# GpSimd splits four fifths of every tap group, SyncE alone moves the first two batches

## The chip, the cores and the metric

The kernel runs on one core of a Trainium2 chip. The metric is the device time of one execution in microseconds (us); the median of three runs before the change is 339.46 us. The question is what the change does to that time.

## The reference, cut to what matters

x has the shape 16 x 128 x 32 x 32 in float32. Two blocks follow each other, each on a group-normalised input, each added to its input:

```
t1 = einsum('nchw,he->ncew', gn(x), p1)                 # 16 rows e out of 32 rows h
t3 = depthwise conv 9x9 of t1 with p3                   # the "taps"
t4 = grouped conv (5 x 1, groups of 4 channels) with p4 # "mix"
t5 = einsum('ncew,ewf->ncf', t4, p5)                    # f = 3 * 128
t6 = depthwise conv of t5 along f with p6
x1 = x + einsum('ncf,nfp->ncp', t6, shifted rows of gn(x)) / sqrt(3c)
out = x1 + relu(batch_norm(1x1 conv of [g2, upsampled Haar details of g2])),  g2 = gn(x1)
```

Products are made at nearly float32 accuracy: each factor is written as a high part (a cast to fp32r) and a rest ("low", the float32 value minus the high part), and three products high x high, high x low, low x high are summed in PSUM.

## The kernel before, in words

The first stage (to about 42 us) loads x, transposes it on VectorE and multiplies it by p1 (`t1`). The second stage, the convolution, runs over 32 channel groups g of four channels. For each group a weight block `s_f` of 128 x 768 is loaded by SyncE's queue (five taps of 128 columns and one mix block of 128 columns), ScalarE casts it to `s_hi` (L516), and the rest `s_lo` is a subtraction. In groups 0 to 13 (`LO_POOL` = 14) GpSimd makes the rest of columns 0 to 511 (`taps_low`, L411) and VectorE that of the other 256 (`split_low`, L859); from group 14 on VectorE makes all 768 columns. Each weight group is split two groups ahead of its use, so in step g of ScalarE and of VectorE group g + 2 is split. `s_lo` and `s_hi` have three buffers, `s_f` has six.

TensorE does for a group fifteen matmuls (L718): ten with `s_hi`, then five with `s_lo`, for which it waits until both parts of the rest are there (`taps_split`). Then come the three mix matmuls of the group before (`t4_product`, L247 to L249, called t4 below), which need `t3_hi` (ScalarE, L558) and `t3_lo` (VectorE, L879) of that group. ScalarE's order within a step g: `t3_hi` of g, evacuation of t4 of g - 1 (L543), the cast `s_hi` of g + 2, and then extras. VectorE's: `t3_lo` of g, the rest of g + 2, extras.

The extras: the evacuated t4 tiles are regrouped by transfers from SBUF to SBUF (`shuffle`, L302) in four batches of 9, 9, 9 and 5 groups, 16 blocks each, and then split (`d_high` on ScalarE L551 or on GpSimd L407; `d_low` on VectorE L868, 128 x 612). For batches 0 to 2 SyncE issues 8 blocks and GpSimd 8, for batch 3 it is 7 and 9. SyncE does so in its loop of weight loads, for batch 0 in its steps 18 to 21 and for batch 1 in steps 27 to 30, two blocks in each; its step g waits for the rest of group g - 6 before it loads the weights of group g. ScalarE's first `d_high` of batch 0 stands in step 15, that of batch 1 in step 25, and each waits for the whole batch (`wait_d`). Other extras are the statistics of x on VectorE (L840, L892, L898, and the group averages, one matmul L728 on TensorE ahead of the next group), the split of p5 (`p5_lo`, L911), a power -1/2 on GpSimd (L437) and the forms of the 1x1 weights on GpSimd (`w_forms`, L417 to L422).

After group 31 batches 2 and 3 are split: all four pieces of each on ScalarE and VectorE. TensorE bridges this time with matmuls that only keep its clock (L750), and then starts the product with p5 (`t5_product`), whose first part needs twelve pieces of the first three batches and the first of batch 3. The third stage runs over the 16 images, and the last one applies the batch normalisation and stores.

Of the kernel before, what the change touches and what calls it, by code (L numbers as in the profile page):

```python
# [38 lines left out]
NB, GB = 4, 9  # L39
# [11 lines left out]
WR, SR = 6, 3  # L51
# [1 line left out]
BY_ACT = 1  # L53
ACT_STATS = {2: (0, 0), 5: (0, 1)}
EARLY = 8
LO_POOL, LO_COLS = 14, 4 * C
AGGR_AT, ST1_AT, GST_AT = 13, 17, 20
P5_AT, P5_LO_AT = 7, {9: 0, 10: 1, 11: 2, 12: 3}
P5_RAW_AT = 6
W_RAW_AT, W_DET_AT = 21, 16  # L60
SHUFFLE_AT = (18, 27)
SHUFFLE_POOL_AT = 10
PER_STEP = 2
SP_BLOCKS, LAST_SP = 8, 7
D_HI_AT = {15: (0, 0), 18: (0, 1), 20: (0, 2), 22: (0, 3), 25: (1, 0), 28: (1, 1)}
D_HI_POOL = ((1, 2), (1, 3))
D_LO_AT = {16: (0, 0), 19: (0, 1), 21: (0, 2), 23: (0, 3), 26: (1, 0), 27: (1, 2), 29: (1, 1), 30: (1, 3)}
D_HI_ACT = list(D_HI_AT.values()) + [(b, piece) for b in (NB - 2, NB - 1) for piece in range(CI)]


def build(nc, x, p1_blk_in, taps_in, p5_in, p6, w_in, gamma, beta, out):
    ctx = ExitStack()
    with ctx:
# [218 lines left out]

        def wait_d(eng, b):

            by_pool = len(blocks) - (SP_BLOCKS if b < NB - 1 else LAST_SP)
            eng.wait_ge(d_in[b], 16 * (len(blocks) - by_pool))
            eng.wait_ge(d_in_pool[b], 16 * by_pool)

        def shuffle(eng, b, some, done):
            groups = FIRST[b + 1] - FIRST[b]  # L300
            for jl, co in some:
                eng.dma_start(  # L302
                    d_sb[b][32 * jl:32 * jl + 32, co].rearrange("p g j n -> p (g j n)"),
                    t4_out[32 * co:32 * co + 32, b % 2, jl, 0:groups].rearrange("p g j n -> p (g j n)")
                    ).then_inc(done, 16)

        def d_ready(eng, b):

            eng.wait_ge(s["t4_ev"], FIRST[b + 1])
            eng.wait_ge(s["conv"], d_groups[b])  # L310

        @block.sync
        def _(sp):
# [17 lines left out]
            def shuffle_step(step):  # L331

                for b in range(NB - 2):
                    i = PER_STEP * (step - SHUFFLE_AT[b])
                    if i == 0:
                        d_ready(sp, b)
                    if 0 <= i < SP_BLOCKS:
                        shuffle(sp, b, blocks[i:i + PER_STEP], d_in[b])

            for g in range(3, G):  # L340
# [8 lines left out]
                    sp.wait_ge(s["p5_lo"], JC)  # L349
                    sp.dma_start(w_raw[:, :, :], w_in).then_inc(s["w_raw"], 16)  # L350
            d_ready(sp, NB - 2)
            shuffle(sp, NB - 2, blocks[:SP_BLOCKS], d_in[NB - 2])
            sp.wait_ge(s["d_lo"], CI)
            sp.wait_ge(s["conv"], x_groups)
            reload_x(sp, 0)
# [15 lines left out]
        def _(pool):  # L371
# [42 lines left out]
            def w_forms():  # L414
                pool.wait_ge(s["w_det"], 1)
                w1, w2, w3, minus_w1 = (w_det[:, k, :] for k in range(4))
                pool.tensor_tensor(w_f[:, 1, :], w2, w3, ALU.add)  # L417
                link(pool.tensor_tensor(w_f[:, 3, :], w2, w3, ALU.subtract))
                pool.tensor_tensor(w_f[:, 2, :], w1, w_f[:, 1, :], ALU.subtract)
                link(pool.tensor_tensor(w_f[:, 4, :], minus_w1, w_f[:, 3, :], ALU.subtract))  # L420
                pool.tensor_tensor(w_f[:, 1, :], w1, w_f[:, 1, :], ALU.add)
                pool.tensor_tensor(w_f[:, 3, :], minus_w1, w_f[:, 3, :], ALU.add).then_inc(s["w_f"], 1)  # L422

            def two_blocks(b, i):
                shuffle(pool, b, blocks[SP_BLOCKS + 2 * i:SP_BLOCKS + 2 * i + 2], d_in_pool[b])
# [410 lines left out]
        def _(dve):  # L836
# [281 lines left out]
```

## Time and profile before

| what | value |
|---|---|
| three runs | 338.56, 339.46, 340.72 us |
| the profiled execution, its time | 337.9 us |
| its span, first to last instruction | 336.1 us |
| mean granted TensorE clock | 0.927 |
| TensorE matmul busy | 274.3 us (82%) |
| VectorE busy | 277.9 us (83%) |
| ScalarE busy | 231.4 us (69%) |
| GpSimd busy | 207.2 us (62%) |

The times of single instructions below are of the profiled execution, in us from the start of its span; 1.8 us of its time lie outside the span. Busy shares are averages over stages with different limits, so the argument goes by the rows of the convolution.

### The profile page before, as it was taken

The numbers are of one execution on the slowest core, as the hardware profiler recorded it, in microseconds if no ns is written. First come the engines' busy times: TensorE is split into PE (matmuls) and PEld (weight loads), VectorE is DVE, ScalarE is ACT, GpSimd is POOL, SyncE is SP. The second block draws the span as 40 slices with busy tenths as digits, with TensorE's granted clock in tenths as the row PEclk, the third lists the DMA queues.
The fourth block names the chain that finished last, engine by engine and source line by source line (L and its number), as shares of the span: only waits on it lengthen the run. The fifth ranks groups of instructions, "written<-read, shape, count | busy, mean of one in ns | idle before, by whom it ended". The sixth has DMA issues, their size and how long they took to land.

```text
span 336.1 us, 4816 instructions
## 1 busy us (share of the span) xinstructions
PE 274.3 (82%) x1544; PEld 226.7 (67%) x1544; DVE 277.9 (83%) x541; ACT 231.4 (69%) x353; POOL 207.2 (62%) x203
## 2 busy tenths in 40 slices
PE   3576599979899889999999999999999998871000
PEld 0111189979799885878888998988889997750000
DVE  3899878997779697768789999999999999765992
ACT  0797838855787657547657778787777787464990
POOL 7398866790029915215878888888898888642000
PEclk9978969998999999999999999999999999987555
DMA  8999456577668376792000000000000000000599
GB/s 216 313 319 277 160 194 184 186 206 208 194 197 245 83 231 168 277 412 102 2 0 3 0 1 2 0 0 2 0 4 1 0 2 0 0 0 1 234 405 360
DMA packets 15096, 43.59 MB, mean 130 GB/s; under 512 B 3056, under 2 KB 3280, under 8 KB 15072
## 3 DMA queue, kind: packets, MB, share of 16 engines
q1 hardware_dynamic: 12672, 36.83, 33.2%
q10 hardware_dynamic: 1344, 4.20, 4.3%
q0 software_dynamic: 1056, 2.27, 2.3%
q8 instruction: 12, 0.20, 0.2%
q14 instruction: 12, 0.10, 0.1%
HBM read 30.44 MB, written 8.39 MB: 116 GB/s over the span
## 4 chain that ended last, share of the span: by engine, by line
PE 54%; DVE 18%; ACT 8%; POOL 6%; DMA 5%; issue 5%; SPq 1%; DVEq 0%; POOLq 0%; ACTq 0%
PE wide L718 10%; PE wide L247 9%; PE wide L249 8%; PE wide L248 8%; DVE xa L853 5%; DVE x_sb L1066 5%; PE bank L795 4%; PE bank L247 4%; PE bank L249 3%; PE bank L248 3%; DMA x_slot<-in_x 3%; DMA d_sb<-t_out 2%; PE bank L799 2%; DVE s_lo L859 2%; DVE d_split L868 2%
## 5 line engine op out<-in xcount | busy, mean ns | idle before, releaser
L718 PE MATMUL wide<-t_all,s_hi 128*128 128x272 f32 (+1 forms) x320 | 47.5, 297 | 2.2 <-ACT t_all L507 1.4
L718 PEld LDWEIGHTS wide<-t_all,s_hi 128*128 128x128 f32 x320 | 43.9, 202 | 3.5 <-ACT t_all L507 2.3
L475 POOL TENSOR_TENSOR g_lo<-y_sb,g_hi 128x1024 fp32r<-128x1024 f32 x15 | 36.1, 2409 | 14.5 <-ACT y_sb L645 14.5
L451 POOL TENSOR_TENSOR g_lo<-y_sb,g_hi 128x1024 fp32r<-128x1024 f32 x15 | 36.0, 2399 | 12.1 <-ACT g_hi L605 12.1
L247 PE MATMUL wide<-g_hi,t_hi 128*128 128x512 f32 x96 | 37.5, 390 | 0.3 <-DVE t_lo L985 0.3
L249 PE MATMUL wide<-g_hi,t_lo 128*128 128x512 f32 x96 | 37.6, 392 | 0.0
L248 PE MATMUL wide<-g_lo,t_hi 128*128 128x512 f32 x96 | 37.4, 390 | 0.0
L853 DVE STREAM_TRANSPOSE xa<-x_slot 128x1024 f32<-128x1024 f32 x16 | 31.3, 2023 | 6.9 <-DMA x_slot<-in_x 6.2
L644 ACT ACTIVATE g_hi<-x_sb,rs 128x1024 fp32r<-128x1024 f32 x16 | 21.3, 1330 | 19.9 <-POOL rs L460 19.9
L859 DVE TENSOR_TENSOR s_lo<-s_f,s_hi 128x768 fp32r<-128x768 f32 (+1 forms) x32 | 25.5, 796 | 9.9 <-ACT s_hi L516 9.7
L302 POOL DMA_DIRECT2D d_sb<-t_out x33 | 16.6, 508 | 26.3 <-ACT t_out L543 26.1
L397 POOL TENSOR_TENSOR t_all<-t_f,t_all 128x512 fp32r<-128x512 f32 x17 | 26.0, 1556 | 8.8 <-ACT t_f L510 8.7
L686 PE MATMUL bank<-xa,p_blk 128*64 128x512 f32 x64 | 21.2, 754 | 10.5 <-DVE xa L853 7.9
L516 ACT CAST s_hi<-s_f 128x768 fp32r<-128x768 f32 x32 | 26.7, 834 | 0.0
L958 DVE TENSOR_TENSOR x_sb<-x_sb,wide 128x512 f32<-128x512 f32 x32 | 21.7, 678 | 5.8 <-PE wide L249 5.8
L558 ACT CAST t_hi<-wide 128x272 fp32r<-128x272 f32 x32 | 12.6, 393 | 19.5 <-PE wide L718 19.5
L718 PE MATMUL wide<-t_all,s_lo 128*128 128x272 f32 (+1 forms) x160 | 25.6, 291 | 0.1
L247 PE MATMUL bank<-p_hi,d_split 128*128 128x384 f32 x68 | 24.6, 362 | 0.7 <-DVE d_split L868 0.7
L411 POOL TENSOR_TENSOR s_lo<-s_f,s_hi 128x512 fp32r<-128x512 f32 x14 | 20.4, 1459 | 7.9 <-ACT s_hi L516 7.8
L686 PEld LDWEIGHTS bank<-xa,p_blk 128*64 128x64 f32 x64 | 3.8, 154 | 28.5 <-DVE xa L853 28.0
L249 PE MATMUL bank<-p_hi,d_split 128*128 128x384 f32 x68 | 23.0, 338 | 0.0
L248 PE MATMUL bank<-p_lo,d_split 128*128 128x384 f32 x68 | 22.9, 337 | 0.0
(136 smaller groups left out, 833.7 us busy)
## 6 DMA issues: line engine op xcount, KB each, us to landing
s_f<-in_taps SPq DMA_DIRECT2D x32, 384.0 KB, 4.0
x_sb<-in_x SPq DMA_DIRECT2D x8, 1024.0 KB, 8.0
out<-x_sb SPq DMA_DIRECT2D x7, 1024.0 KB, 5.1
x_slot<-in_x ACTq DMA_DIRECT2D x12, 256.0 KB, 13.5
x_slot<-in_x SPq DMA_DIRECT2D x12, 256.0 KB, 14.1
d_sb<-t_out POOLq DMA_DIRECT2D x24, 76.5 KB, 3.3
d_sb<-t_out SPq DMA_DIRECT2D x24, 76.5 KB, 3.2
x_slot<-in_x ACTq DMA_DIRECT2D x8, 128.0 KB, 4.6
```

Source lines behind the costliest of these rows:

```text
L247: nc.tensor.matmul(ps, w[0], m[0], start=start, stop=False)
L248: nc.tensor.matmul(ps, w[0], m[1], start=False, stop=False)
L249: return nc.tensor.matmul(ps, w[1], m[0], start=False, stop=stop)
L397: pool.tensor_tensor(t1[:, :, 1, 2:2 + J, at].rearrange("p g j -> p j g"), t1_f[i % 2][:, :, :], t1[:, :, 0, 2:2 + J, at].bitcast(F32).rea ...
L451: pool.tensor_tensor(g1_lo[:, W:W + HW], y_sb[:, n, :], g1_hi[:, W:W + HW].bitcast(F32), ALU.subtract).then_inc(s["g1_lo"], 1)
L475: pool.tensor_tensor(g2_lo[:, :], y_sb[:, n, :], g2_hi[:, :].bitcast(F32), ALU.subtract).then_inc(s["g2_lo"], 1)
L516: act.copy(s_hi[:, g % SR, :], s_f[:, g % WR, :]).then_inc(s["s_hi"], 1)
L686: mm = pe.matmul(ps_t1[i % 4][64 * v:64 * v + 64, :], p1_blk[:, :], rhs, start=True, stop=True)
L718: mm = pe.matmul(ps_t3[g % 2][:, j0 * NO:j1 * NO], weights[:, g % SR, 128 * t:128 * t + 128], t1_all[:, row + j0:row + j1, :].rearrange("p ...
L853: dve.transpose(xa[:, n % 2], x_slot[n // 2][:, n % 2, :].rearrange("p (h w) -> p w h", w=W)).then_inc(s["xa"], 1)
L859: dve.tensor_tensor(s_lo[:, g % SR, first:], s_f[:, g % WR, first:], s_hi[:, g % SR, first:].bitcast(F32), ALU.subtract).then_inc(s["s_lo" ...
L958: dve.tensor_tensor(x_sb[:, n, sl], x_sb[:, n, sl], ps_o[:, sl], ALU.add).then_inc(s["x1"], 1)
```

## The change

GpSimd's loop `for g in range(G)` now covers all 32 groups of `taps_low`; VectorE makes the rest of columns 512 to 767 alone, in all groups. SyncE issues all 16 blocks of batches 0 and 1, four in each of its steps 18 to 21 and 27 to 30. GpSimd's other work is put into its loop: `w_forms` behind group 23, the two `d_high` behind groups 27 and 29, the power behind group 30; its shares of batches 2 and 3 come behind the loop. The aggregation of the statistics moves from step 13 to 17, its last part from 17 to 21 (TensorE's average from ahead of group 19 to ahead of group 23), the factors from 20 to 24; `p5_lo` from steps 9 to 12 to steps 12 to 15; the load of the 1x1 weights from SyncE's step 21 to 24 and their scaling on ScalarE from step 16 to 19; `d_low` of piece (1, 2) from step 27 to 28.

```diff
-LO_POOL, LO_COLS = 14, 4 * C
-AGGR_AT, ST1_AT, GST_AT = 13, 17, 20
-P5_AT, P5_LO_AT = 7, {9: 0, 10: 1, 11: 2, 12: 3}
+LO_COLS = 4 * C
+AGGR_AT, ST1_AT, GST_AT = 17, 21, 24
+P5_AT, P5_LO_AT = 7, {12: 0, 13: 1, 14: 2, 15: 3}
 P5_RAW_AT = 6
-W_RAW_AT, W_DET_AT = 21, 16
+W_RAW_AT, W_DET_AT = 24, 19
 SHUFFLE_AT = (18, 27)
-SHUFFLE_POOL_AT = 10
-PER_STEP = 2
-SP_BLOCKS, LAST_SP = 8, 7
+PER_STEP = 4
+SP_BLOCKS, LAST_SP = (16, 16, 8), 7
+POW_AT, W_FORMS_AT = 30, 23
 D_HI_AT = {15: (0, 0), 18: (0, 1), 20: (0, 2), 22: (0, 3), 25: (1, 0), 28: (1, 1)}
-D_HI_POOL = ((1, 2), (1, 3))
-D_LO_AT = {16: (0, 0), 19: (0, 1), 21: (0, 2), 23: (0, 3), 26: (1, 0), 27: (1, 2), 29: (1, 1), 30: (1, 3)}
+D_HI_POOL_AT = {27: (1, 2), 29: (1, 3)}
+D_HI_POOL = list(D_HI_POOL_AT.values())
+D_LO_AT = {16: (0, 0), 19: (0, 1), 21: (0, 2), 23: (0, 3), 26: (1, 0), 28: (1, 2), 29: (1, 1), 30: (1, 3)}
...
-            eng.wait_ge(s["s_lo_pool"], min(g + 1, LO_POOL))
+            eng.wait_ge(s["s_lo_pool"], g + 1)
...
-            for g in range(LO_POOL):
+            for g in range(G):
                 taps_low(g)
-                if g == SHUFFLE_POOL_AT:
-                    d_ready(pool, 0)
-                if g >= SHUFFLE_POOL_AT:
-                    two_blocks(0, g - SHUFFLE_POOL_AT)
-            d_ready(pool, 1)
-            for i in range(2):
-                two_blocks(1, i)
-            pool.wait_ge(s["gst"], 1)
-            pool.tensor_tensor(rs1[:, 1, :], rs1[:, 0, :], minus_half[:, :].broadcast_to([128, N]),
-                               ALU.pow).then_inc(s["gst_q"], 1)
-            for i in range(2, 4):
-                two_blocks(1, i)
-            w_forms()
-            for b, co in D_HI_POOL:
-                d_high(b, co)
-            d_ready(pool, 2)
-            shuffle(pool, 2, blocks[SP_BLOCKS:], d_in_pool[2])
-            d_ready(pool, 3)
-            shuffle(pool, 3, blocks[LAST_SP:], d_in_pool[3])
+                if g in D_HI_POOL_AT:
+                    d_high(*D_HI_POOL_AT[g])
+                if g == W_FORMS_AT:
+                    w_forms()
+                if g == POW_AT:
+                    pool.wait_ge(s["gst"], 1)
+                    pool.tensor_tensor(rs1[:, 1, :], rs1[:, 0, :], minus_half[:, :].broadcast_to([128, N]),
+                                       ALU.pow).then_inc(s["gst_q"], 1)
+            d_ready(pool, NB - 2)
+            shuffle(pool, NB - 2, blocks[SP_BLOCKS[NB - 2]:], d_in_pool[NB - 2])
+            d_ready(pool, NB - 1)
+            shuffle(pool, NB - 1, blocks[LAST_SP:], d_in_pool[NB - 1])
...
             def split_low(g):
-                first = LO_COLS if g < LO_POOL else 0
                 dve.wait_ge(s["s_hi"], g + 1)
-                dve.tensor_tensor(s_lo[:, g % SR, first:], s_f[:, g % WR, first:],
-                                  s_hi[:, g % SR, first:].bitcast(F32), ALU.subtract).then_inc(s["s_lo"], 1)
+                dve.tensor_tensor(s_lo[:, g % SR, LO_COLS:], s_f[:, g % WR, LO_COLS:],
+                                  s_hi[:, g % SR, LO_COLS:].bitcast(F32), ALU.subtract).then_inc(s["s_lo"], 1)
```

## Rows read from the trace of the kernel before

**Rows 1.** Stretches: from:to us, length, busy us of TensorE, its weight loads, VectorE, ScalarE, GpSimd; granted clock; DMA.

```profile
75.00:79.00 4.00, 3.96 (x19) 3.96 (x20) 3.47 (x7) 1.12 (x2) 0.15 (x1) 0.57 0.93 257
79.00:125.00 46.00, 42.59 (x330) 40.42 (x328) 36.16 (x66) 33.81 (x64) 19.11 (x25) 1.00 0.66 194
150.00:280.00 130.00, 129.13 (x709) 114.93 (x708) 116.97 (x294) 96.90 (x142) 108.92 (x93) 1.00 0.03 12
```

**Rows 2.** TensorE's timeline in the convolution: start, length, engine, what, idle before.

```profile
48.37 0.29 PE L247 MATMUL wide<-t_hi,s_hi 128*128 128x272 f32 x1
...
67.45 0.76 PE L718 MATMUL wide<-t_all,s_lo 128*128 128x272 f32 x5
68.05 0.30 PE L247 MATMUL wide<-t_hi,s_hi 128*128 128x272 f32 x1
...
75.05 0.58 PE L247 MATMUL wide<-t_hi,s_hi 128*128 128x272 f32 x1 [1.85 <-DVE t_lo L879]
...
78.88 0.29 PE L247 MATMUL wide<-t_hi,s_hi 128*128 128x272 f32 x1
...
87.84 0.39 PE L247 MATMUL wide<-t_hi,s_hi 128*128 128x272 f32 x1
...
91.32 0.39 PE L247 MATMUL wide<-t_hi,s_hi 128*128 128x272 f32 x1 [0.95 <-DVE t_lo L879]
...
94.60 0.29 PE L247 MATMUL wide<-t_hi,s_hi 128*128 128x272 f32 x1
...
123.62 0.39 PE L247 MATMUL wide<-t_hi,s_hi 128*128 128x272 f32 x1
...
134.33 0.41 PE L247 MATMUL bank<-p_hi,d_split 128*128 128x384 f32 x1 [0.74 <-DVE d_split L868]
```

**Rows 3.** VectorE's timeline, the columns as before.

```profile
68.54 1.60 DVE L911 TENSOR_TENSOR p_lo<-p_raw,p_hi 128x384 fp32r<-128x384 f32 x1
...
70.42 1.85 DVE L859 TENSOR_TENSOR s_lo<-s_f,s_hi 128x256 fp32r<-128x256 f32 x1
...
74.92 0.41 DVE L859 TENSOR_TENSOR s_lo<-s_f,s_hi 128x256 fp32r<-128x256 f32 x1
...
75.85 0.54 DVE L911 TENSOR_TENSOR p_lo<-p_raw,p_hi 128x384 fp32r<-128x384 f32 x1
...
100.98 0.96 DVE L859 TENSOR_TENSOR s_lo<-s_f,s_hi 128x768 fp32r<-128x768 f32 x1
101.86 1.42 DVE L868 TENSOR_TENSOR d_split<-d_sb,d_split 128x612 fp32r<-128x612 f32 x1
...
127.47 5.04 DVE L868 TENSOR_TENSOR d_split<-d_sb,d_split 128x612 fp32r<-128x612 f32 x4 [1.49 <-ACT d_split L551]
```

**Rows 4.** GpSimd's timeline.

```profile
65.45 1.53 POOL L411 TENSOR_TENSOR s_lo<-s_f,s_hi 128x512 fp32r<-128x512 f32 x1 [0.66 <-ACT s_hi L516]
...
68.42 1.30 POOL L411 TENSOR_TENSOR s_lo<-s_f,s_hi 128x512 fp32r<-128x512 f32 x1
...
100.65 2.95 POOL L437 TENSOR_TENSOR rs<-rs,minus_half 128x16 f32<-128x16 f32 x1 [6.00 <-DVE rs L905]
...
109.55 0.46 POOL L420 TENSOR_TENSOR w_f<-w_det,w_f 128x128 f32<-128x128 f32 x1
...
126.57 4.39 POOL L302 DMA_DIRECT2D d_sb<-t_out  x9 [7.84 <-ACT t_out L543]
```

**Rows 5.** SyncE's queue in order of time.

```profile
81.98 1.49 SPq L302 DMA_DIRECT2D d_sb<-t_out  x2
...
114.53 5.23 SPq L302 DMA_DIRECT2D d_sb<-t_out  x8
```

**Rows 6.** ScalarE's timeline, step 15 and the last split.

```profile
85.72 1.30 ACT L551 CAST d_split<-d_sb 128x612 fp32r<-128x612 f32 x1 [0.75 <-DMA d_sb<-t_out]
...
126.17 4.45 ACT L551 CAST d_split<-d_sb 128x612 fp32r<-128x612 f32 x4
```

**Rows 7.** The chain of waits in order of time: start, length, what.

```profile
130.47 2.04 DMA d_sb<-t_out
```

More of the change, by code:

```diff
@@ L293, in wait_d @@
         def wait_d(eng, b):
-            by_pool = len(blocks) - (SP_BLOCKS if b < NB - 1 else LAST_SP)
+            by_pool = len(blocks) - (SP_BLOCKS[b] if b < NB - 1 else LAST_SP)
             eng.wait_ge(d_in[b], 16 * (len(blocks) - by_pool))
-            eng.wait_ge(d_in_pool[b], 16 * by_pool)
+            if by_pool:
+                eng.wait_ge(d_in_pool[b], 16 * by_pool)
         def shuffle(eng, b, some, done):
@@ L336, in shuffle_step @@
                         d_ready(sp, b)
-                    if 0 <= i < SP_BLOCKS:
+                    if 0 <= i < SP_BLOCKS[b]:
                         shuffle(sp, b, blocks[i:i + PER_STEP], d_in[b])
@@ L351, in _ @@
             d_ready(sp, NB - 2)
-            shuffle(sp, NB - 2, blocks[:SP_BLOCKS], d_in[NB - 2])
+            shuffle(sp, NB - 2, blocks[:SP_BLOCKS[NB - 2]], d_in[NB - 2])
             sp.wait_ge(s["d_lo"], CI)
@@ L422, in w_forms @@
                 pool.tensor_tensor(w_f[:, 3, :], minus_w1, w_f[:, 3, :], ALU.add).then_inc(s["w_f"], 1)
-            def two_blocks(b, i):
-                shuffle(pool, b, blocks[SP_BLOCKS + 2 * i:SP_BLOCKS + 2 * i + 2], d_in_pool[b])
-            for g in range(LO_POOL):
+            for g in range(G):
                 taps_low(g)
-                if g == SHUFFLE_POOL_AT:
-                    d_ready(pool, 0)
-                if g >= SHUFFLE_POOL_AT:
-                    two_blocks(0, g - SHUFFLE_POOL_AT)
-            d_ready(pool, 1)
-            for i in range(2):
-                two_blocks(1, i)
-            pool.wait_ge(s["gst"], 1)
-            pool.tensor_tensor(rs1[:, 1, :], rs1[:, 0, :], minus_half[:, :].broadcast_to([128, N]),
-                               ALU.pow).then_inc(s["gst_q"], 1)
-            for i in range(2, 4):
-                two_blocks(1, i)
-            w_forms()
-            for b, co in D_HI_POOL:
-                d_high(b, co)
-            d_ready(pool, 2)
-            shuffle(pool, 2, blocks[SP_BLOCKS:], d_in_pool[2])
-            d_ready(pool, 3)
-            shuffle(pool, 3, blocks[LAST_SP:], d_in_pool[3])
+                if g in D_HI_POOL_AT:
[10 more added lines that the diff above has]
+            shuffle(pool, NB - 1, blocks[LAST_SP:], d_in_pool[NB - 1])
             def g1_low(n):
```

## The prediction

> **What bounds the kernel now.** I read the stretches first. In the third stage TensorE is busy 129.13 of 130 us [rows 1], so whatever delay the convolution leaves behind is carried to the end undiminished, and nothing of the change touches that stage. So only the convolution counts, and there TensorE's timeline says what a group costs: from the t4 at 48.37 to the one at 68.05 lie nine groups, 2.19 us each, with no gaps [rows 2]. That is the floor. The t4 at 48.37 follows group 1 and that at 123.62 group 31: thirty intervals, 75.25 us, against 65.6 at the floor. So 9.6 us are lost in waits. They lie in three places. Between 68.05 and 78.88 three groups took 10.83 instead of 6.56: 4.3 lost. From 87.84 to 94.60 two took 6.76: 2.4 lost (0.95 of it VectorE's `t3_lo`, then a stop of TensorE for the group averages). From 94.60 to 123.62 twelve took 29.02 instead of 26.24: 2.8 lost.
>
> The cause of the first loss is in VectorE's timeline. A p5 rest that takes 0.54 alone took 1.60 at 68.54, a 256-column rest that takes 0.41 took 1.85 at 70.42 [rows 3]. GpSimd had begun its own subtraction at 68.42 and ended it at 69.72 [rows 4]; the p5 rest ended 0.42 after that. So a VectorE operation with two inputs in SBUF stands still while GpSimd's subtraction runs. `t3_lo`, with one input in PSUM, is queued behind it and comes late, TensorE waits 1.85 us at 75.05 [rows 2], and the granted clock falls: 0.57 in the stretch after, nearer the 1.2 GHz level than the 2.4 [rows 1]. The other way round GpSimd loses: at 65.45, with VectorE's 256 columns ahead, its 512 columns took 1.53 instead of 1.30 [rows 4].
>
> **A group after the change.** I lay it out on a clean one, t4 at time 0 (68.05 minus 4.37 is 63.68). The cast `s_hi` is there at 1.75, GpSimd's rest runs 1.77 to 3.30 (65.45 and its 1.53), and TensorE wants it at 3.77 (67.45). So GpSimd has 0.5 of slack before the need, and 2.19 - 1.53 = 0.66 idle per group. `t3_lo` of the next group must be done by 4.37.
>
> **Part 1: the first loss goes.** GpSimd no longer issues transfers between subtractions, so it stays in phase and VectorE's 256 columns go first. The p5 rests move to steps 12 to 15: each waits for GpSimd to 3.30, ends near 3.8, and `t3_lo` ends at 4.1, in time by 0.25. I take nothing for it; without that margin it costs up to 0.3 in each of four groups. The t4 after group 17, at 87.84 before, could then come at 68.05 + 7 x 2.19 = 83.4.
>
> **Part 2: batch 0 comes no earlier.** SyncE's step 18 waits for the rest of group 12, GpSimd's now, at 68.05 + 3.30 = 71.35. Then it has 16 blocks and four weight loads to issue alone. Eight blocks took it 5.23 us, 0.65 each [rows 5]; twenty issues at that are 13.1 and the last block starts at 83.8, landing 2.04 later [rows 7] at 85.8. At 0.49 each, GpSimd's price (4.39 for nine [rows 4]), it would be about 82.7. I take 85.2, near SyncE's own row, as a weight load is one shorter issue. ScalarE's step 15 waits for the whole batch, as it did till 85.72 [rows 6], with the `t3_hi` behind it. From the start of that cast to t4 it was 87.84 - 85.72 = 2.12, so t4 comes at 87.3 instead of 83.4. TensorE stands for 3.9 us, longer than the 1.85 after which the clock fell, so the next interval is like that from 75.05 to 78.88, 3.83 instead of 2.19 [rows 2]. The t4 after group 18 lies at 91.1 against 91.32: **-0.2**, for a part that removed 4.3 (bounds -2.7 for landing at 82.7 and the clock falling all the same, +0.4 for 85.8). The weight loads queued behind the blocks are not late: they are issued six groups ahead, and SyncE falls back by some 2 us.
>
> **Part 3: the group averages.** Before, 94.60 - 91.32 - 2.19 = 1.1 were lost there. Their last VectorE step now stands in step 21 behind the 256 columns, and GpSimd's subtraction of that step runs to 3.4; the tiny operations have two SBUF inputs too, so they end near 3.8, and TensorE, which wants the result at 2.57, loses 1.3 and a matmul's 0.3. **+0.5** (from -0.7, if operations on 15 columns don't wait, to +1).
>
> **Part 4: `d_low` against GpSimd.** Eight steps hold a `d_low`, 1.26 on VectorE (four in 5.04; 1.42 recorded for one in the loop), 1.3 with the gap. Before, VectorE did 0.88 (100.98 to 101.86) + 1.3 + 0.4 of work (`t3_lo` is 272 columns, taken like the 256-column 0.41) [rows 3], and with the wait for `s_hi` a step fitted barely. Now the cover is gone: 256 columns to 2.1, GpSimd to 3.3, `d_low` to 4.6, `t3_lo` to 5.0, against 4.37: 0.6 late, and 0.9 where ScalarE's own cast in the step before made `s_hi` late by about 0.3 (an estimate: that cast is 1.30 long [rows 6], and ScalarE idles (46 - 33.81) / 21 = 0.6 a group with its casts included [rows 1]). Were `d_low` to go first, GpSimd would end at 4.7 against 3.77: 0.9. The first one, step 16, hides under the slow clock of part 2, those of 21, 23 and 30 under parts 3, 5 and 6 in most of their length; four remain, 3.3 us. Batch 1, gated by the rest of group 24 and again 16 issues of SyncE, adds about 1.0 at step 25. Against the 2.8 lost there before: **+1.5** (from -2.8, all hidden, to +4, eight at 0.9).
>
> **Part 5: `w_forms` behind group 23.** Six operations of 0.46 [rows 4] are 2.8; less 0.66 and 0.5 the next rest is late by **+1.6** (0 if TensorE is late by other things just then; 3 if they alternate with VectorE). The two `d_high`, about 1.3 each like ScalarE's [rows 6], exceed the 0.66 idle by about the slack: 0.
>
> **Part 6: the power behind group 30.** 2.95 [rows 4], late by 1.8 for the rest of group 31, partly under step 29's delay: **+1.3** (0 to 2.3).
>
> By the Trainium skill, "SBUF — State Buffer", section "Who interferes with whom", GpSimd shares VectorE's second port pair, and whoever starts first holds it for its whole instruction against the other. The 0.54 that became 1.60 agrees. The power does not: VectorE's 768 columns at 100.98 took 0.96 inside its 2.95 [rows 3, 4]. By the rule the power would stop VectorE as well and the sum would be some 2 us more; by the row nothing is added.
>
> **Part 7: the tail.** GpSimd's transfers of batch 2 lay under the convolution; now they stand behind the rest of group 31. Call its end X. Eight issues at 0.49, so batch 2 is landed at X + 5.9 (last issue starting at X + 3.4, 2.5 to land, an estimate from 2.04 for a block of five groups instead of nine); VectorE's four pieces start 1.3 later and take 5.04 [rows 3], ScalarE's 4.45 [rows 6] lie beside them; the first of batch 3, with 340 of 612 columns, 0.7; TensorE starts at X + 13.1. Batch 3 itself, nine more issues, lands at X + 9.9, in time. Before, TensorE started at 134.33 [rows 2], and the rest of group 31 was needed at about 122.9, so X + 11.4: **+1.7** (0 if X is early, 3.4 if the clock also falls in the gap behind the bridging matmuls).
>
> **The sum.** -0.2 + 0.5 + 1.5 + 1.6 + 1.3 + 1.7 = +6.4. On the profiled 337.9 that is 344.3; the median of the runs is 1.56 above the profile, so **345.9**.
>
> **Rivals.** *Everything hidden, faster.* VectorE gets rid of 18 x 0.54 = 9.7 us of work in a stage where it is often last. If it and GpSimd really ran side by side, all waits after group 18 vanish (1.1 + 2.8) with up to 2.7 of part 2: -4 to -6.6, about 334.5. The rows of 68.54 and 70.42 speak against it; chance 0.08. *Not slower: the delays overlap.* A step late for one reason forgives the next; if one step's slack absorbs parts 3, 5 and 6, what stays is 1.5 + 1.7 - 0.2 - 1.1, or with `d_low` at half its price nothing: it decides whether `d_low` gets the port ahead of GpSimd while GpSimd has slack from a late TensorE. 338 to 342.8, say 341; chance 0.24. *Worse: the clock.* If TensorE falls to the lower level again after the averages and in the tail, each fall costs the 1.64 of 75.05, and parts 4 and 5 at their upper ends add 3: 351; chance 0.15. *The change doesn't do what it says*: all sixteen blocks and all groups follow from the constants, so only if SyncE is no slower issuing (0.49) does part 2 differ; within the above. The forecast has 0.53.
>
> **Chances and range.** Within 1% is about what a measurement of this kernel can tell from no change: 336.1 to 342.9. Faster 0.07, same 0.24, slower 0.69. The range 339 to 352 leaves out the first rival and the ends of the second and third.
>
> **What would show it.** Right: in the profile after, the intervals from 68.05 to the t4 after group 16 are 2.19 each; ScalarE then waits several us for `d_sb` and that step's `d_high` starts at 84 to 86; the granted clock falls there; `d_low` has durations near 2.5 with GpSimd's L411 in between; gaps before L249's `s_lo` or L718's after `w_forms` and the power; GpSimd's last transfers end more than 8 us after its last L411. Wrong: if `d_low` stays at 1.4 while GpSimd's subtractions stay at 1.5, part 4 falls; if the batch lands by 82, part 2 does; if the rest of group 31 is there before 121, part 7 as well.

## The result, and the profile after

The changed kernel takes 347.15 us (median of 4 runs, 345.09 to 351.19), the kernel before 339.01 (4 runs); the ratio is 1.0202, 95% interval 1.0150 to 1.0254. It is slower by 2.0%, and the interval lies above the 1% that the prediction took for no change. The ratios here and below compare fast executions alone, which leaves the 351.19 out. The forecast was 345.9. The profiled execution took 346.64, with a span of 344.9 where the kernel before had 336.1: 8.8 more.

Where do the 8.8 lie? TensorE's timeline of the changed kernel, with L250 the last of the three mix matmuls t4 and L710 the taps' matmuls:

```profile
50.32 0.29 PE L250 MATMUL wide<-t_hi,s_lo 128*128 128x272 f32 x1
...
83.13 0.29 PE L250 MATMUL wide<-t_hi,s_lo 128*128 128x272 f32 x1
...
90.94 0.43 PE L250 MATMUL wide<-t_hi,s_lo 128*128 128x272 f32 x1
...
94.36 0.29 PE L250 MATMUL wide<-t_hi,s_lo 128*128 128x272 f32 x1
...
105.44 0.41 PE L720 MATMUL bank<-mv,g_from 128*128 128x32 f32 x2 [1.07 <-DVE mv L890]
...
110.38 0.84 PE L710 MATMUL wide<-t_all,s_lo 128*128 128x272 f32 x5 [1.09 <-POOL s_lo L413]
...
130.79 1.15 PE L710 MATMUL wide<-t_all,s_lo 128*128 128x272 f32 x5 [2.55 <-POOL s_lo L413]
...
133.51 0.43 PE L250 MATMUL wide<-t_hi,s_lo 128*128 128x272 f32 x1
```

The chain of waits gives the start of the product with p5:

```profile
134.28 2.10 DMA d_sb<-t_out
...
137.73 5.81 DVE d_split L859 x5
...
143.68 0.41 PE bank L248
```

I measure each kernel from its first t4 to its first product with p5 (134.33 [rows 2], 143.68 here). A t4 is timed from here on by the last of its three matmuls, L250 here and L249 in the kernel before, whose first and last are these:

```profile
48.63 0.28 PE L249 MATMUL wide<-t_hi,s_lo 128*128 128x272 f32 x1
...
125.57 0.28 PE L249 MATMUL wide<-t_hi,s_lo 128*128 128x272 f32 x1
```

The stretch takes 85.7 before, 93.4 here, 7.7 more. The first t4 itself came 1.7 later. That is scatter of the loads, not the change: in the other kernels of this study, whose code is the same up to there, it lies between 48.3 and 51.6. Behind the first product with p5 201.7 us are left before and 201.2 here, 0.5 less.

Up to the t4 at 83.13 fifteen intervals take 32.81 us, 2.19 each: the 4.3 of the kernel before are gone. What ate them stands at the next t4. ScalarE's timeline and SyncE's queue of the changed kernel:

```profile
88.34 1.22 ACT L543 CAST d_split<-d_sb 128x612 fp32r<-128x612 f32 x1 [5.95 <-DMA d_sb<-t_out]
```

```profile
73.55 2.48 SPq L304 DMA_DIRECT2D d_sb<-t_out  x4
76.13 0.53 SPq L286 DMA_DIRECT2D s_f<-in_taps  x1
...
83.66 2.71 SPq L304 DMA_DIRECT2D d_sb<-t_out  x4
```

ScalarE stands 5.95 us before batch 0, where it stood 0.75 [rows 6], since SyncE issues the blocks one after the other till 86.4. The stretches of the changed kernel (columns as in [rows 1]) show the granted clock at the full level where it had fallen before, and fallen where it had not:

```profile
75.00:79.00 4.00, 4.00 (x35) 4.00 (x34) 3.33 (x6) 2.62 (x6) 2.69 (x3) 1.00 0.80 253
84.00:95.00 11.00, 5.91 (x37) 5.70 (x36) 5.12 (x8) 4.56 (x10) 3.69 (x2) 0.84 0.56 175
125.00:135.00 10.00, 6.68 (x35) 5.50 (x34) 5.71 (x12) 2.47 (x6) 9.99 (x11) 0.83 0.49 152
```

The clock falls a second time, in the last of these stretches, behind the 2.55 us that TensorE stands for the rest of group 31.

Then VectorE and GpSimd, side by side, in the changed kernel:

```profile
103.72 1.25 DVE L889 TENSOR_TENSOR rs<-mv 128x15 f32<-128x15 f32 x1
...
118.41 2.43 DVE L859 TENSOR_TENSOR d_split<-d_sb,d_split 128x612 fp32r<-128x612 f32 x1
...
123.50 2.48 DVE L859 TENSOR_TENSOR d_split<-d_sb,d_split 128x612 fp32r<-128x612 f32 x1
...
126.58 1.39 DVE L859 TENSOR_TENSOR d_split<-d_sb,d_split 128x612 fp32r<-128x612 f32 x1
...
128.24 1.28 DVE L859 TENSOR_TENSOR d_split<-d_sb,d_split 128x612 fp32r<-128x612 f32 x1
```

```profile
124.68 4.10 POOL L434 TENSOR_TENSOR rs<-rs,minus_half 128x16 f32<-128x16 f32 x1
128.77 1.87 POOL L413 TENSOR_TENSOR s_lo<-s_f,s_hi 128x512 fp32r<-128x512 f32 x1
130.59 8.57 POOL L304 DMA_DIRECT2D d_sb<-t_out  x17
```

The reader sees `d_low` (L859) at 2.43 and 2.48 instead of 1.42 [rows 3] (five of its eight in the loop take 2.03 to 2.49), an operation on 15 columns at 1.25, the power (L434) at 4.10 instead of 2.95 [rows 4], and the 17 transfers of batches 2 and 3 in one piece behind GpSimd's last rest.

What each t4 interval has over 2.19, by where it stands (t4 after group n; one column for each kernel, us):

| place | before | after | difference |
|---|---|---|---|
| groups 11 to 14 | 4.26 | 0.0 | -4.3 |
| 17, 18: batch 0, clock, `d_low` | 1.60 | 6.85 | +5.25 |
| group averages | 0.98 | 1.54 | +0.6 |
| weight forms, group 24 | 0 | 1.31 | +1.3 |
| the other intervals: `d_low` steps and batch 1 | 2.85 | 3.28 | +0.4 |
| power and the `d_low` beside it, group 31 | 0 | 3.29 | +3.3 |
| last t4 to the product with p5, with the last interval | 8.2 | 9.3 | +1.1 |

The differences sum to 7.7 but for rounding.

### The profile page after: what moved, and what is told of

It reads as the page before. It is cut to its first block, busy times and chain, and to the rows that moved or that the text cites. A ratio compares the mean times of both kernels' runs of the same rounds, so it can differ in the third digit from the quotient of the medians.

```text
span 344.9 us, 4824 instructions
## 1 busy us (share of the span) xinstructions
PE 274.5 (80%) x1544; PEld 227.0 (66%) x1544; DVE 279.7 (81%) x541; ACT 231.4 (67%) x353; POOL 228.9 (66%) x205
## 4 chain that ended last, share of the span: by engine, by line
PE 53%; DVE 11%; POOL 10%; DMA 8%; ACT 6%; issue 5%; SPq 4%; DVEq 0%; POOLq 0%; ACTq 0%
PE wide L710 9%; PE wide L248 9%; PE wide L250 8%; PE wide L249 8%; DMA x_slot<-in_x 7%; DVE x_sb L1057 5%; PE bank L787 4%; PE bank L248 3%; PE bank L250 3%; PE bank L249 3%; POOL s_lo L413 2%; SPq L282 2%; PE bank L791 2%; DVE d_split L859 2%; POOL g_lo L467 1%
## 5 line engine op out<-in xcount | busy, mean ns | idle before, releaser
L413 POOL TENSOR_TENSOR s_lo<-s_f,s_hi 128x512 fp32r<-128x512 f32 x32 | 49.1, 1537 | 26.1 <-ACT s_hi L508 26.1
L710 PE MATMUL wide<-t_all,s_hi 128*128 128x272 f32 (+1 forms) x320 | 47.3, 297 | 2.7 <-ACT t_all L499 2.1
L710 PEld LDWEIGHTS wide<-t_all,s_hi 128*128 128x128 f32 x320 | 44.0, 202 | 3.9 <-ACT t_all L499 3.0
L250 PE MATMUL wide<-g_hi,t_lo 128*128 128x512 f32 x96 | 37.5, 391 | 0.0
L249 PE MATMUL wide<-g_lo,t_hi 128*128 128x512 f32 x96 | 37.4, 389 | 0.0
L678 PE MATMUL bank<-xa,p_blk 128*64 128x512 f32 x64 | 22.7, 802 | 9.4 <-DVE xa L845 9.2
L850 DVE TENSOR_TENSOR s_lo<-s_f,s_hi 128x256 fp32r<-128x256 f32 x32 | 23.0, 720 | 8.6 <-ACT s_hi L508 8.4
L710 PE MATMUL wide<-t_all,s_lo 128*128 128x272 f32 (+1 forms) x160 | 25.8, 293 | 3.9 <-POOL s_lo L413 3.9
L859 DVE TENSOR_TENSOR d_split<-d_sb,d_split 128x612 fp32r<-128x612 f32 (+1 forms) x16 | 23.8, 1534 | 4.1 <-ACT d_split L543 4.1
L710 PEld LDWEIGHTS wide<-t_all,s_lo 128*128 128x128 f32 x160 | 22.2, 197 | 4.7 <-issue 4.7
L870 DVE TENSOR_TENSOR t_lo<-wide,t_hi 128x272 fp32r<-128x272 f32 x32 | 13.8, 433 | 11.3 <-ACT t_hi L550 11.1
L250 PE MATMUL bank<-p_hi,d_split 128*128 128x384 f32 x68 | 23.0, 338 | 0.0
```

What stands on the lines that cost most here:

```text
L249: nc.tensor.matmul(ps, w[0], m[1], start=False, stop=False)
L250: return nc.tensor.matmul(ps, w[1], m[0], start=False, stop=stop)
L413: pool.tensor_tensor(s_lo[:, g % SR, 0:LO_COLS], s_f[:, g % WR, 0:LO_COLS], s_hi[:, g % SR, 0:LO_COLS].bitcast(F32), ALU.subtract).then_in ...
L710: mm = pe.matmul(ps_t3[g % 2][:, j0 * NO:j1 * NO], weights[:, g % SR, 128 * t:128 * t + 128], t1_all[:, row + j0:row + j1, :].rearrange("p ...
L850: dve.tensor_tensor(s_lo[:, g % SR, LO_COLS:], s_f[:, g % WR, LO_COLS:], s_hi[:, g % SR, LO_COLS:].bitcast(F32), ALU.subtract).then_inc(s[ ...
L859: dve.tensor_tensor(lo, src, hi.bitcast(F32), ALU.subtract).then_inc(s["d_lo"], 1)
```

## The experiments

Each was timed beside the kernel before; a ratio is to it. "To p5" is the time from the first t4 to the first product with p5 in the profiled execution (85.7 before, 93.4 changed).

| run | median us | ratio (95%) | to p5 |
|---|---|---|---|
| e1, batch 0 split later | 343.61 | 1.0127 (1.0072 to 1.0181) | 90.6 |
| e2, old transfers | 347.67 | 1.0261 (1.0212 to 1.0310) | 94.1 |
| e3, VectorE alone from group 14 | 342.03 | 1.0090 (1.0055 to 1.0125) | 89.6 |
| e4, SyncE issues batch 2 | 347.25 | 1.0238 (1.0192 to 1.0284) | 93.7 |
| c1 = e1 + e3 | 336.17 | 0.9886 (0.9851 to 0.9922) | 86.0 |
| c2, kernel before, p5 rests moved | 338.80 | 0.9979 (0.9952 to 1.0007) | 85.7 |
| e5, power on one column | 348.59 | 1.0256 (1.0207 to 1.0304) | 93.5 |
| e5b, e5 + reload held | 345.55 | 1.0187 (1.0151 to 1.0224) | 92.0 |
| e6b, GpSimd writes, reads nothing | 350.55 | 1.0333 (1.0294 to 1.0372) | 95.0 |
| e8, e6b shorter + reload held | 343.69 | 1.0157 (1.0108 to 1.0205) | 90.1 |
| e7, p5 rests in steps 9 to 12 | 347.94 | 1.0269 (1.0209 to 1.0330) | 94.0 |
| c3, c1 with another bridge | 335.17 | 0.9887 (0.9848 to 0.9925) | 83.3 |

**e1: ScalarE splits batch 0 later.**

```diff
-D_HI_AT = {15: (0, 0), 18: (0, 1), 20: (0, 2), 22: (0, 3), 25: (1, 0), 28: (1, 1)}
+D_HI_AT = {18: (0, 0), 20: (0, 1), 22: (0, 2), 24: (0, 3), 26: (1, 0), 28: (1, 1)}
-D_LO_AT = {16: (0, 0), 19: (0, 1), 21: (0, 2), 23: (0, 3), 26: (1, 0), 28: (1, 2), 29: (1, 1), 30: (1, 3)}
+D_LO_AT = {19: (0, 0), 21: (0, 1), 23: (0, 2), 25: (0, 3), 27: (1, 0), 28: (1, 2), 29: (1, 1), 30: (1, 3)}
```

> The changed kernel with the splits of batch 0 on ScalarE in steps 18, 20, 22, 24 instead of 15, 18, 20, 22 (batch 1's first in 26 instead of 25) and VectorE's a step later each, so that ScalarE doesn't stand before batch 0. My sum: the 5.95 us wait at step 15 goes, TensorE keeps its pace to group 18 (5.3 us earlier than in the changed kernel, clock included), and the splits stand closer together, which gives back 1 to 2: 342 to 344. Rival 'GpSimd's added rests are the whole cost': the wait was harmless, 346 to 348. Rival 'SyncE's issues are the whole cost': 339 to 341.

343.61. The first twenty t4 are 2.19 apart; the one after group 20 lies 41.6 behind the first, 48.4 in the changed kernel. So the wait cost 6.9 us at that point. But only 2.8 reach the p5 product: the splits stand closer together now, GpSimd's rests are still there, and the stretch behind loses more (3.6 at the t4 after group 23, ahead of which the averages stand, 1.7 after group 27, 3.6 after group 31). It takes both: run c1 below has the same splits without those rests and loses 5.4 from the t4 after group 20 to that after group 31, where e1 loses 13.9. The wait for batch 0 is a real cost, and not the whole one.

**e2: transfers of batches 0 and 1 as before the change.**

```diff
-PER_STEP = 4
-SP_BLOCKS, LAST_SP = (16, 16, 8), 7
+PER_STEP = 2
+SP_BLOCKS, LAST_SP = (8, 8, 8), 7
+POOL_BLOCKS_AT = {10: 0, 21: 1}
...
+                for first, b in POOL_BLOCKS_AT.items():
+                    if g == first:
+                        d_ready(pool, b)
+                    if first <= g < first + 4:
+                        i = 8 + 2 * (g - first)
+                        shuffle(pool, b, blocks[i:i + 2], d_in_pool[b])
```

> The changed kernel with the transfers of batches 0 and 1 shared as before (SyncE 8 blocks in four steps, GpSimd two blocks behind each of its rests 10 to 13 and 21 to 24); GpSimd still makes its rest in all groups. My sum: the loss at groups 11 to 13 comes back (about 4), batch 0 is landed at about the same time, the loss behind it is smaller for that, GpSimd gets 4 more us of issues in the crowded steps 21 to 24: 346 to 350. Rival 'SyncE's issues are the whole cost': 338 to 341. Rival 'GpSimd's added rests are the whole cost': 346 to 348 too, but then with no loss near group 11.

347.67. The rival "SyncE's issues are the whole cost" falls: without them the time is the same. The loss at the t4 after group 17 shrinks from 5.6 to 2.6, and GpSimd's transfers in steps 21 to 24 give it back (3.5 and 1.5 where the changed kernel has 1.3 and 0.2). One thing I had not expected: groups 11 to 14 lose 0.6, not 4, although GpSimd's transfers stand between its rests again. Runs c2 and e7 below settle that.

**e3: VectorE makes all 768 columns from group 14 on.**

```diff
-            eng.wait_ge(s["s_lo_pool"], g + 1)
+            eng.wait_ge(s["s_lo_pool"], min(g + 1, LO_POOL))
...
-                taps_low(g)
-                if g in D_HI_POOL_AT:
-                    d_high(*D_HI_POOL_AT[g])
+                if g < LO_POOL:
+                    taps_low(g)
+                if g == POW_AT:
+                    for b, co in D_HI_POOL:
+                        d_high(b, co)
                 if g == W_FORMS_AT:
                     w_forms()
-                if g == POW_AT:
+                if g == W_FORMS_AT + 1:
...
+                first = LO_COLS if g < LO_POOL else 0
```

GpSimd's forms, power and two `d_high` follow each other here with no rest between or behind them.

> The changed kernel with the rests from group 14 on made by VectorE alone in 768 columns, as before the change; the transfers stay with SyncE, GpSimd's other work keeps its order without the rests between. My sum: the wait for batch 0 stays with its fallen clock (the t4 after group 18 lies 1.0 us later than in the kernel before, counted from the start of the convolution), of the 5.6 us lost behind it and the 1.1 of the tail nearly all goes: 339 to 342. Rival 'SyncE's issues are the whole cost': 346 to 348. Rival 'GpSimd's added rests are the whole cost': 336 to 339.

342.03, 5 less than the changed kernel, at the edge of what my sum gave. Behind the t4 after group 18 the intervals lose 5.1 in all instead of 9.4, and the wait for batch 0 stays (ScalarE's timeline of e3):

```profile
88.97 1.22 ACT L545 CAST d_split<-d_sb 128x612 fp32r<-128x612 f32 x1 [6.38 <-DMA d_sb<-t_out]
```

GpSimd's added rests, with what its other work does by standing between them, are worth 5 us of the time, and what is left above the kernel before is 3: neither theory of a single cause holds.

**e4: SyncE issues batch 2 whole.**

```diff
-SP_BLOCKS, LAST_SP = (16, 16, 8), 7
+SP_BLOCKS, LAST_SP = (16, 16, 16), 7
...
-            d_ready(pool, NB - 2)
-            shuffle(pool, NB - 2, blocks[SP_BLOCKS[NB - 2]:], d_in_pool[NB - 2])
```

> The changed kernel with SyncE issuing all 16 blocks of batch 2 as well, so that GpSimd has only its nine of batch 3 behind its last rest. The tail term of my sum is 1.7 (1.1 in the profile after): TensorE's first product with p5 starts about 1 us earlier against its last t4, the time is 345 to 346.5. Rival: the tail is bound by the last t4 and ScalarE's splits, which stay: no change, within 0.3 us of the changed kernel.

347.25, no change. The chain of waits of e4:

```profile
130.50 5.14 DMA x_sb<-in_x
...
135.68 10.07 PE bank L740 x24
```

SyncE's reload of x, which stands behind the sixteen blocks in its queue, now comes at 130.5, and the matmuls that bridge the gap read x. The reload makes them wait only 0.12 behind the last t4, but they run in part at a fallen clock (granted 0.51 from 133 to 140) and take 10.07. Even so they hold the product with p5 up by no more than about 0.3: it starts 0.43 behind VectorE's fifth piece, and 0.15 behind it in the changed kernel. The rest is in ScalarE's timeline of e4:

```profile
135.88 4.40 ACT L541 CAST d_split<-d_sb 128x612 fp32r<-128x612 f32 x4
143.18 2.90 ACT L541 CAST d_split<-d_sb 128x340 fp32r<-128x340 f32 x4 [2.90 <-DMA d_sb<-t_out]
```

Batch 2 is early, and ScalarE now stands 2.90 for batch 3, whose blocks can be issued only behind the last t4. GpSimd issued its last one at 140.46, 0.04 behind SyncE's second reload of x, and it took 2.64 to land instead of 2.0. From the last t4 to the product with p5 it is 10.17, as in the changed kernel. So the rival had it in the main: the last t4 bounds the tail, though through batch 3 and not through the number of ScalarE's casts. Without that block's 0.6 and the bridge's 0.3 the tail would be 0.9 shorter, the 1 us that I expected (an estimate from these times).

**c1: e1 and e3 together.** The diffs are those above.

> Both undone together: the late splits of batch 0 (first run of the study) and VectorE's 768 columns from group 14 (third run), SyncE still issuing batches 0 and 1 whole. My sum: no wait at step 15, no fallen clock, no loss near group 11; behind group 18 the losses of the kernel before (about 4) and 1 more for the splits that stand closer: TensorE starts its product with p5 81 to 83 us behind its first t4 (85.7 before, 93.4 changed), the time is 334 to 337, 2 to 4 below the kernel before. Rival 'the splits need the spread that steps 15 to 22 gave them': what the wait cost comes back, 338 to 341.

336.17, ratio 0.9886: faster than the kernel before. The last t4 lies 72.6 behind the first (76.9 before, 83.2 changed). But to p5 it is 86.0, not 81 to 83. The chain of waits of c1 says why:

```profile
114.58 9.14 DMA x_sb<-in_x
...
123.76 11.02 PE bank L744 x24
```

```profile
123.76 11.02 PE L744 MATMUL bank<-x_sb,g_mean 128*128 128x384 f32 x24 [2.63 <-DMA x_sb<-in_x]
```

The reload took 9.14 us to land, the bridge began 2.63 us after TensorE fell idle (its timeline is the second fence), and 24 matmuls took 11.02. VectorE's fifth piece was done at 131.23, 3.1 before the product with p5, where 0.15 lie between them in the changed kernel: the bridge costs 2.9 here.

**c2: the kernel before with only the p5 rests moved.**

```diff
-P5_AT, P5_LO_AT = 7, {9: 0, 10: 1, 11: 2, 12: 3}
+P5_AT, P5_LO_AT = 7, {12: 0, 13: 1, 14: 2, 15: 3}
```

> The kernel before with one edit, the p5 rests in steps 12 to 15 instead of 9 to 12. As my prediction had it, the early loss of 4.3 came from GpSimd's transfers between its rests: then it stays here, 338 to 340. The second run of the study speaks for a rival: with those transfers kept and the p5 rests moved, groups 11 to 14 lost 0.6 only, so the p5 rests had to meet them. Then the loss shrinks to about 1; batch 0 is gated by the rest of group 15, which comes earlier too: 335 to 337.

338.80, ratio 0.9979 (0.9952 to 1.0007): no difference. Yet groups 11 to 14 lose 0.5 instead of 4.3. The t4 after group 17 then loses 4.2 for batch 0 instead of 0.3, and ScalarE stands 4.79 instead of 0.75:

```profile
88.18 1.22 ACT L551 CAST d_split<-d_sb 128x612 fp32r<-128x612 f32 x1 [4.79 <-DMA d_sb<-t_out]
```

This is the cleanest sight of a gain given back: batch 0 is the bound there, and what stands ahead of it can be made shorter for nothing.

**e7: the changed kernel with the p5 rests in steps 9 to 12.** The edit is that of c2, backwards.

> The changed kernel with the p5 rests back in steps 9 to 12; GpSimd issues no transfers there. If the early loss needs both, GpSimd's transfers between its rests and the p5 rests in the same steps, groups 11 to 13 lose under 0.3 us in all and the time is that of the changed kernel, 346 to 348. If the place of the p5 rests alone makes the loss, 2 to 4 us are lost before group 13; the wait for batch 0 behind it swallows them, and the time is the same too, so the trace decides.

347.94, as the changed kernel. Groups 11 to 14 lose 1.1, more than my 0.3 and far less than 4.3. VectorE's timeline of e7:

```profile
69.61 1.04 DVE L902 TENSOR_TENSOR p_lo<-p_raw,p_hi 128x384 fp32r<-128x384 f32 x1
...
70.93 1.54 DVE L850 TENSOR_TENSOR s_lo<-s_f,s_hi 128x256 fp32r<-128x256 f32 x1
```

Both operations wait for GpSimd once, but not time after time. With GpSimd's transfers alone (c2) the loss is 0.5, with the p5 rests there alone (e7) it is 1.1, with both (before) 4.3. Apart from these two, e7 differs from the kernel before in other places too (the aggregation in step 17 instead of 13, for one), so its 1.1 is a looser figure than the 0.5 of c2. (In e7 GpSimd's last block of batch 3 went out 0.11 behind SyncE's reload and took 4.1 to land; e5 below has the same at length.)

**e5: the power on one column.** The other 15 factors are left at one.

```diff
+            pool.memset(rs1[:, 1, :], 1.0)
-                    pool.tensor_tensor(rs1[:, 1, :], rs1[:, 0, :], minus_half[:, :].broadcast_to([128, N]),
+                    pool.tensor_tensor(rs1[:, 1, 0:1], rs1[:, 0, 0:1], minus_half[:, :],
```

> The changed kernel with the power on one column of the 16 (the other 15 factors are left at one, so they are left out of the computation); behind group 30 stand about 0.6 us on GpSimd instead of 4.1. My term for the power was 1.3 and the trace has 3.3 lost before the last group: the loss at the last t4 but one falls to about 1 or less, and the time by 2.3 to 3.3: 344 to 345. Rival 'the loss there is VectorE's, with three d_low in a row': no change, 347.

348.59, not less. The loss before group 31 fell as expected, from 3.29 to 1.24, but to p5 it is 93.5, as in the changed kernel (93.4). The chain of waits of e5:

```profile
129.27 7.36 POOL d_sb L304 x15
136.63 5.00 DMA d_sb<-t_out
...
141.71 0.78 ACT d_split L544
```

and SyncE's queue:

```profile
131.78 4.31 SPq L304 DMA_DIRECT2D d_sb<-t_out  x7
136.19 12.61 SPq L277 DMA_DIRECT2D x_sb<-in_x  x7
```

SyncE's second reload of x, 1024 KB, is issued at 136.19, ahead of GpSimd's last small block at 136.63, and that block takes 5.00 us to land. In the changed kernel the last block went out just before the reload (138.7 against 138.81) and nothing waited.

Then 1.4 us more are lost behind the product with p5. TensorE stood 2.86 us ahead of it, and its granted clock fell; the first row is e5, the second the changed kernel:

```profile
145.00:150.00 5.00, 5.00 (x22) 5.00 (x23) 1.81 (x5) 1.97 (x3) 1.75 (x1) 0.71 0.74 248
...
145.00:150.00 5.00, 5.00 (x29) 4.79 (x29) 2.82 (x8) 2.10 (x4) 2.00 (x1) 1.00 0.62 212
```

Four runs have this loss: in e5, e6b, e7 and e8 TensorE stood 2.55 to 3.72 us ahead of the product and 202.6 to 202.9 us were left behind it. In the ten other profiles it stood 1.65 at most, and 201.1 to 201.7 were left.

**e5b: e5 with that reload held back.** 15 of the 16 factors are still left at one.

```diff
-            sp.wait_ge(s["d_lo"], 2 * CI)
-            reload_x(sp, 1)
             sp.wait_ge(s["d_lo"], NB * CI)
-            for k in range(2, N // 2):
+            for k in range(1, N // 2):
```

> The run with the power on one column (15 of 16 factors left at one, left out of the computation), and SyncE's second reload of x, 1024 KB, held back until all d_low are done, so that it can't be ahead of GpSimd's last block of batch 3, which took 5.00 us to land in that run. My sum, mended: what the short power gave at group 31 (2.05) now reaches TensorE; its first product with p5 starts 90.5 to 91.5 us behind the first t4 (93.51 without the hold, 93.36 in the changed kernel), the time is 344.5 to 346.5. Rival 'VectorE's eight d_low at the end bound the start whatever lands': 93 again, 347 to 349.

345.55, 92.0 to p5; no block of batch 3 takes over 2.5 us to land. So the long power is worth 2.0 at group 31 and 1.4 at the p5 product, once the reload is out of its way. The ratios alone (1.0187 here, 1.0202 for the change) don't tell the two kernels apart.

**e6b: GpSimd writes and doesn't read.**

```diff
-                pool.tensor_tensor(s_lo[:, g % SR, 0:LO_COLS], s_f[:, g % WR, 0:LO_COLS],
-                                   s_hi[:, g % SR, 0:LO_COLS].bitcast(F32), ALU.subtract).then_inc(s["s_lo_pool"], 1)
+                for k in range(3):
+                    ins = pool.memset(s_lo[:, g % SR, 0:LO_COLS].bitcast(F32), 0.0)
+                    if k < 2:
+                        link(ins)
+                ins.then_inc(s["s_lo_pool"], 1)
```

> The changed kernel with GpSimd writing zeros three times over its 512 columns, about 1.6 us in all, instead of subtracting (the rest of four of five taps is left out of the computation): GpSimd is as busy but reads nothing from SBUF there. My account of the port: VectorE's d_low goes back from 2.4 to 1.3-1.4 and its 256 columns from 1.2 to 0.4 wherever they meet GpSimd's writes, the losses at the d_low steps go (about 3), the wait for batch 0, the forms and the power stay: 343 to 345. Rival 'GpSimd is late by its own length, the port has no part': 346 to 348 and d_low stays at 2.4.

350.55, outside both. The mechanism is plain in VectorE's and GpSimd's timelines of e6b:

```profile
103.19 0.17 DVE L892 TENSOR_TENSOR rs<-mv 128x15 f32<-128x15 f32 x1
...
118.72 1.40 DVE L862 TENSOR_TENSOR d_split<-d_sb,d_split 128x612 fp32r<-128x612 f32 x1
...
123.23 1.40 DVE L862 TENSOR_TENSOR d_split<-d_sb,d_split 128x612 fp32r<-128x612 f32 x1
```

```profile
118.53 3.41 POOL L414 MEMSET s_lo<- 128x512 f32 x6
```

`d_low` takes 1.40 while GpSimd writes, and 1.29 to 1.43 in all eight steps; it took 2.43 while GpSimd subtracted. The operation on 15 columns takes 0.17 instead of 1.25. The averages lose 0.38 (1.54), the `d_low` steps 0.35, 0.60 and 0.15 (0.97, 1.33, 0.76). The time went up all the same, for three reasons outside the port: three writes take 1.70, longer than a subtraction, so that the forms cost 2.3 and 1.5; the reload overtook GpSimd's last block again (5.54 to land); and TensorE stood 3.72 ahead of the product with p5, behind which 1.5 us more were lost as in e5.

**e8: two writes, and the reload held.** The edits are those of e6b with `range(2)` and of e5b.

> The run with GpSimd writing zeros instead of subtracting, now twice over the 512 columns (about 1.1 us, a bare subtraction takes 1.3) and with SyncE's second reload of x held back until all d_low are done (the rest of four of five taps is left out of the computation). My account: with neither the port nor the reload in the way, the d_low steps lose under 0.5 each, the forms and the power still block GpSimd but shorter, TensorE starts its product with p5 89.5 to 91 us behind the first t4 (93.36 changed, 94.96 with three writes and no hold), the time is 342.5 to 345. Rival 'length and place of GpSimd's work, not the port': 92 to 93.5, 346 to 347.

343.69, 90.1 to p5, as my account had it, with 1.7 us more behind the product with p5 than in the changed kernel. This run changes three things (port, length, reload), so it prices the port only together with them; that the port acts, and on which operations, is shown by the durations in e6b.

**c3: c1 with a bridge that doesn't read x.**

```diff
-WARM, WARM_LAST = 12, 3
+WARM, WARM_LAST = 15, 3
-                    pe.matmul(bank[:, 0:NF], g_mean[:, :, :].rearrange("p a b -> p (a b)"), x_sb[:, 0, 0:NF],
+                    pe.matmul(bank[:, 0:NF], g_mean[:, :, :].rearrange("p a b -> p (a b)"), p5_hi[:, 0, :].bitcast(F32),
-            pe.wait_ge(x_in[0], 16 * CI + 16)
+            pe.wait_ge(s["p5_hi"], JC)
```

> Both parts undone as in the version that was faster than the kernel before, and the bridging matmuls read p5_hi, which is long there, instead of the reloaded x, and are 30 instead of 24. There the reload took 9.14 us to land, TensorE stood 2.6 us, its clock fell and the bridge took 11.02 us, 1 to 3 us longer than the splits needed. My sum: the bridge follows the last t4 at once at the full clock, TensorE starts its product with p5 82.5 to 84 us behind the first t4 (86.04 there), the time is 332 to 335. Rival 'the splits of batch 3 bound the start anyway': 85.5 to 86, 335 to 337.

335.17, ratio 0.9887. To p5 it is 83.3, 2.8 less than c1. The chain of c3 has the bridge right behind the last t4, 30 matmuls in less time than the 24 of c1, and from the last t4 to the product with p5 it is 9.5 instead of 13.5:

```profile
122.75 9.68 PE bank L744 x30
```

The last t4 itself lies 1.2 later than in c1, since the t4 after groups 21 and 22 lose 2.5 more, at a granted clock of 0.78 from 91 to 98; no edit of c3 explains that. The times don't show those 2.8: the ratios of c1 and c3 are equal (0.9886 and 0.9887, intervals of 0.7%), the medians differ by 1.0. Whether c3 is faster than c1 stays open; both are faster than the kernel before by 1.1%.

## Why the prediction was right

The sign, the size (7.7 in the stretch that the change touches, 6.4 forecast) and most places were right. That the sum came within 1.3 is in part luck: parts 2, 3 and 6 were too low by 3.3 in all, parts 4, 5 and 7 too high by 2.0. By its parts:

- **Part 1**: the first loss did vanish, and moving the p5 rests cost nothing. My cause was half of it. I put it down to GpSimd's transfers, and it takes these and the p5 rests together (4.3 against 0.5 and 1.1 alone).
- **Part 2**: forecast -0.2, measured +1.0 at the t4 after group 18 (44.0 against 43.05 behind the first). SyncE's issues took 12.8 us from 73.55 to 86.37; less the 1.7 by which the convolution began later that is 84.7, where 0.65 each had given 84.4. I had picked a time between this and GpSimd's cheaper price, and the last block took 2.54 to land instead of 2.04 (that row is a block of five groups; part 7 allows 2.5 for one of nine, and part 2 should have too): batch 0 was there at 86.7 on the old scale, above my upper bound of 85.8. That the gain of 4.3 is eaten here is shown by c2, in the kernel before, and by e1 from the other side.
- **Part 3**: +0.5 forecast, +0.6 measured, and for the reason given: 1.25 for an operation on 15 columns, 0.17 where GpSimd doesn't read (e6b).
- **Part 4**: +1.5 forecast, +0.4 measured. The uncovered `d_low` lost what I had worked out (0.97, 1.33, 0.76, three instead of four, 3.1 instead of 3.3), but batch 1 made ScalarE wait only 0.35 and cost next to nothing instead of 1.0, and what the kernel before lost there was nearly as much.
- **Part 5**: +1.6 forecast, +1.3 measured.
- **Part 6**: +1.3 forecast, +3.3 measured, the term that was sized worst. I took 2.95 for the power and let half a microsecond be forgiven by a late TensorE. It took 4.10: begun at 124.68, it stood until `d_low` ended (123.50 + 2.48 = 125.98) and then took 2.8. The rest behind it took 1.87, since the `d_low` of 128.24 had begun before it. With the power short 1.2 are left (e5), so 2.0 are the power's and the others come from VectorE's `d_low` in the same steps, which the forecast had hidden under it.
- **Part 7**: +1.7 forecast. From the last t4 (L250 at 133.51, L249 at 125.57) to the p5 product it is 10.2 against 8.8, +1.4; with the last interval, shorter by 0.3 after a late one, +1.1. The order that I had (batch 2's landing, five pieces on VectorE, TensorE) is the chain of the trace, 5.81 for the five pieces.

Of the rivals, the faster one needed VectorE and GpSimd side by side, and they stand in turn. That of the overlapping delays held for batch 1 alone; the averages, the forms and the power each kept their loss. That of the clock expected more falls than one; a second came, but behind the power and not after the averages, and the fall behind the bridging matmuls shows only in e5, e6b, e7 and e8. The rule of the Trainium skill, "SBUF — State Buffer", section "Who interferes with whom", that a VectorE instruction with two SBUF inputs is held up only by a GpSimd one that reads SBUF, agrees with e6b: 1.40 beside writes, 2.43 beside subtractions. Its "for the whole instruction" doesn't hold for the power: at 126.58, in the middle of it, `d_low` took 1.39.

## What to carry to other kernels

Work moved to an idle engine is free only if the two engines can run side by side; look in the trace for an operation of the one that grows by the rest of an operation of the other, and price the move by the turns that they take. When a loss is removed ahead of a transfer that a later step waits for, ask first when that transfer lands: here 4 us were saved twice (the change, c2) and swallowed by batch 0 both times. And a small transfer that goes out just ahead of a large one of another queue can come to stand behind it when the work ahead of either is made shorter or longer (e5, e6b, e7).

## What the runs showed of the hardware

- A VectorE operation with two SBUF inputs and a GpSimd subtraction excluded each other at the small and the large size alike: 15 columns took 1.25 instead of 0.17, 612 columns 2.43 instead of 1.4. GpSimd's writes didn't count (0.17 and 1.40 in e6b).
- The power of GpSimd waits for VectorE's operation to begin, but doesn't hold VectorE up while it runs (4.10 with 1.3 of waiting, `d_low` inside at 1.39; 2.93 in c1, where no two-input operation ran as it began).
- A block of 42.5 KB that was issued 0.44, 0.33, 0.11 and 0.04 us behind a 1024 KB load of another queue took 5.0 (e5), 5.5 (e6b), 4.1 (e7) and 2.6 us (e4) to land; one issued 0.14 ahead of it (the changed kernel) took 2.0.
- TensorE's granted clock fell behind stops of 2.55 (e7), 2.75 (e8), 2.86 (e5) and 3.72 us (e6b) ahead of the product with p5, and 1.4 to 1.7 us were lost there; it did not behind one of 1.65 (the changed kernel).
